# A four-layer diffusion block: two groups of samples per pass of a loop, or four groups in one unrolled wave

## The reference

```python
# L0: ln, modulate, self attention (rope, mask 128x128), gate; ln, cross attention (77 keys, mask), gate; ln, MLP 4x, gate
x = x + g_msa * self_out
x = x + g_x * cross
x = x + g_mlp * (gelu(xm @ W1 + b1) @ W2 + b2)
# L1: ada_ln of x and of the context, cross attention (77 keys)
x = x_q + (out @ Wp + bp)
# L2: self attention gated by gate_msa; cross attention (77 keys); MLP 4x gated by gate_mlp
# L3: nx = ln(x); one-head attention over 77 keys gives evidence
combined = concat(nx, evidence, anchor)
h = silu(combined @ e_w1 + e_b1)              # 3 experts of 256
routed = sum(expert_out * router_probs)
g = sigmoid(silu(combined @ gate_w1 + gate_b1) @ gate_w2 + gate_b2)
x = x + g * (routed @ out_w + out_b)
```

## Time and profile before

| | |
|---|---|
| median of 3 runs | 987.18 us (987.16 to 987.22) |
| the profiled execution | 980.62 us, span 978.7 us |
| mean granted TensorE clock | 0.856 of full |
| PE busy | 780.3 us (80%), 9226 matmuls |
| DVE, ACT, POOL busy | 468.3 us, 325.2 us, 203.1 us |
| instructions | 22436 |

### The profile page before, as it was taken

The page is one execution under the profiler, slowest core; times in us unless marked ns, Lnnn a source line. Parts: engine busy times, 40 slices in busy tenths (PEclk is TensorE's granted clock), DMA queues, the critical chain, the costliest instruction groups (busy, mean ns, idle before and its releaser), DMA issues.

```text
span 978.7 us, 22436 instructions
## 1 busy us (share of the span) xinstructions
PE 780.3 (80%) x9226; PEld 474.7 (49%) x9226; DVE 468.3 (48%) x1111; ACT 325.2 (33%) x544; POOL 203.1 (21%) x239
## 2 busy tenths in 40 slices
PE   5688888787788788868947888878878878887797
PEld 4244444545454455554633445454544445555447
DVE  3557544444455755332146566545344676343403
ACT  0123334233323333325421233352423233224362
POOL 1323221212123322010013233213022223111000
PEclk9799978858778987689979999996777899659899
DMA  8300000000000000000031000000000000000000
GB/s 299 109 1 13 13 1 2 2 1 2 2 2 2 2 2 2 1 0 1 1 109 50 2 3 1 2 1 1 2 1 2 1 2 2 1 2 1 1 0 23
DMA packets 5360, 16.26 MB, mean 17 GB/s; under 512 B 1577, under 2 KB 2612, under 8 KB 4360
## 3 DMA queue, kind: packets, MB, share of 16 engines
q1 hardware_dynamic: 4588, 10.72, 3.3%
q10 hardware_dynamic: 668, 4.05, 1.1%
HBM read 13.66 MB, written 1.09 MB: 15 GB/s over the span
## 4 chain that ended last, share of the span: by engine, by line
PE 65%; ACT 13%; DVE 11%; issue 8%; POOL 1%; DMA 1%; DVEq 0%; SPq 0%; ACTq 0%; POOLq 0%
PE avp L1006 15%; PE lin L889 12%; PE big L981 11%; PE lin L902 10%; ACT P L528 7%; ACT hT L515 4%; PE big L957 3%; DVE mhl L734 2%; PE big L989 2%; PE lin L911 2%; PE big L977 2%; DVE hid L758 2%; PE mtp L963 2%; PE big L974 1%; DVE xn L696 1%
## 5 line engine op out<-in xcount | busy, mean ns | idle before, releaser
L528 ACT ACTIVATE P<-big 77x1024 f32<-77x1024 f32 (+1 forms) x160 | 154.6, 1017 | 406.0 <-PE big L989 406.0
L734 DVE TENSOR_REDUCE mhl<-big 128x8 bf16<-128x616 f32 (+1 forms) x160 | 152.8, 964 | 108.2 <-PE big L957 105.3
L889 PE MATMUL lin<-hT,W 128*128 128x512 f32 x184 | 115.4, 734 | 39.5 <-ACT hT L515 37.0
L469 POOL TENSOR_TENSOR qm<-qT,hm 128x512 f32<-128x512 f32 x80 | 88.6, 1108 | 198.6 <-PE big L989 104.3
L981 PE MATMUL big<-qm,kT 32*77 32x512 f32 (+1 forms) x640 | 111.1, 770 | 0.0
L1006 PE MATMUL avp<-P,Vp 77*32 77x128 f32 (+1 forms) x2560 | 99.7, 304 | 4.0 <-ACT P L528 4.0
L1006 PE MATMUL avp<-P,onesp 77*32 77x128 f32 (+1 forms) x2560 | 101.4, 308 | 0.0
L436 POOL TENSOR_SCALAR rstd<-mv 128x4 f32<-128x4 f32 (+1 forms) x36 | 8.3, 230 | 433.0 <-DVE mv L687 432.8
L957 PE MATMUL big<-kbm,qb 32*128 32x308 bf16 (+1 forms) x320 | 57.4, 359 | 50.4 <-ACT P L528 50.2
L1006 PEld LDWEIGHTS avp<-P,Vp 77*32 77x32 f32 (+1 forms) x2560 | 73.8, 120 | 29.9 <-issue 19.4
L1006 PEld LDWEIGHTS avp<-P,onesp 77*32 77x32 f32 (+1 forms) x2560 | 85.7, 126 | 1.2
(11 more groups left out here) (153 smaller groups left out, 843.2 us busy)
## 6 DMA issues: line engine op xcount, KB each, us to landing
gbc<-gate_rows SPq DMA_DIRECT2D x4, 1280.0 KB, 8.8
W<-in_w ACTq DMA_DIRECT2D x2, 1152.0 KB, 12.3
hid<-in_ws SPq DMA_DIRECT2D x2, 832.0 KB, 5.7
W<-in_w ACTq DMA_DIRECT2D x1, 1088.0 KB, 6.7
xin<-in_x SPq DMA_DIRECT2D x4, 256.0 KB, 4.8
out<-x SPq DMA_DIRECT2D x4, 256.0 KB, 2.2
ctx<-in_ctx SPq DMA_DIRECT2D x4, 154.0 KB
ctxT<-in_ctxT SPq DMA_DIRECT2D x4, 154.0 KB
```

Source lines behind the costliest of these rows:

```text
L469: nc.gpsimd.tensor_tensor(qm[:, j % 2], q.broadcast_to([128, 4, T]), mask.broadcast_to([128, 4, T]), ALU.mult).then_inc(qm_ready, 1)
L528: nc.scalar.activation(P[j % 2][0:kw, 8 * half:8 * half + 8, :], big[0:kw, 2 * half:2 * half + 2, :].rearrange("p g (h q) -> p (g h) q", h=4),
L734: v.tensor_reduce(mhl[:].rearrange("p (g c) -> p g c", c=32)[:, 2 * half:2 * half + 2, 0:4], big[:, 2 * half:2 * half + 2, 0:4 * kw].rearr ...
L889: i = mm(lin_ap(st, s, job, m)[:, 0:n], w, a, start=(c == 0), stop=(c == len(parts) - 1))
```

## The change

The loop is gone: `NS` = 4 groups are in flight, `ITERS` and all turns counted by iteration disappear, and the list `UNITS` is run once. Attention blocks follow each other in `ORDER`, a wave: group 1 begins while group 0 is between its first two blocks, and so on. A chain of side work (`CHAINS`) is laid between two blocks of its group, each unit at a share of the way, over the blocks of the other groups that lie between. `TAILS` lays out the last MLP and the mixture of each group: those of group 0 wholly, of groups 1 and 2 partly, behind attention jobs, the rest behind `END`.

```diff
-NS = 2
-ITERS = B // (GB * NS)
+NS = B // GB
...
+ORDER = [(0, 0), (0, 1), (1, 0), (0, 2), (1, 1), (2, 0), (0, 3), (1, 2), (2, 1), (3, 0),
+         (1, 3), (2, 2), (3, 1), (4, 0), (2, 3), (3, 2), (4, 1), (3, 3), (4, 2), (4, 3)]
+POS = {block: p for p, block in enumerate(ORDER)}
+JOBS = len(ORDER) * GB
+END = 16 * len(ORDER)
...
+CHAINS = [
+    along((0.0, ("l0", "stat")), (0.15, ("l0", "apply")), (0.3, ("l0", "t")), (0.45, ("p0", "k")), (0.7, ("p0", "q")),
+          (1.0, ("p0", "v"))),
+    along((0.0, ("p1", "k"), ("l4", "stat")), (0.1, ("o0", "y")), (0.25, ("l4", "apply")), (0.35, ("l1", "stat"), ("l4", "t")),
+          (0.5, ("p1", "v")), (0.65, ("l1", "apply")), (0.8, ("l1", "t")), (1.0, ("p1", "q"))),
+    along((0.0, ("o1", "y"), ("l2", "stat")), (0.15, ("l2", "apply")), (0.25, ("l2", "t")), (0.35, ("m0", "h0")),
+          (0.38, ("m0", "h1")), (0.42, ("m0", "h2")), (0.46, ("m0", "h3")), (0.56, ("m0", "y"), ("l3", "stat")),
+          (0.6, ("p2", "k")), (0.7, ("p2", "v")), (0.74, ("l3", "apply")), (0.86, ("l3", "t")), (1.0, ("p2", "q"))),
...
+TAILS = [(16 * 14, 16 * 18), (16 * 17, END + 16), (16 * 19, END + 60), (END + 16, END + 76)]
+
+
+def chain_slots(k, s):
+
+    if k == NAT:
+        return TAILS[s]
+    end = 16 * POS[k, s] - 6
+    if k:
+        return 16 * (POS[k - 1, s] + 1), end
+    return max(16 * POS[k, s] - 28, 0), end
...
+def placed():
 
     out = []
+    for s in range(NS):
+        for k, chain in enumerate(CHAINS):
+            if (k, s) == (0, 0):
+                continue
+            first, last = chain_slots(k, s)
+            for share, u in chain:
+                slot = first + round(share * (last - first))
+                if u == (f"p{k}", "v"):
+                    slot = max(slot, values_slot(k, s))
+                    assert slot < 16 * POS[k, s] + 3
+                out.append((slot, u, s))
+    return sorted(out, key=lambda e: e[0])
+
+
+PLACED = placed()
+UNITS = [("B", u, 0) for _, u in CHAINS[0]] + [("START", None, None)]
+for _slot in range(END):
+    UNITS.append(("A", _slot // 4, _slot % 4))
+    UNITS += [("B", u, s) for slot, u, s in PLACED if slot == _slot]
+UNITS += [("END", None, None)] + [("B", u, s) for slot, u, s in PLACED if slot >= END]
```

```diff
+        Vp2 = [sb(f"Vp{i}", [128, GB, H, 32]) for i in range(2)]
+        hid2 = [sb(f"hid{i}", [128, 7, N]) for i in range(2)]
+        Vp, hid = ([pair[s % 2] for s in range(NS)] for pair in (Vp2, hid2))
+        gring = sb("gring", [128, NGB, GB, 128])
...
-        P = [sb(f"P{i}", [128, H, T]) for i in range(2)]
+        P = sb("P", [128, H, T])
...
+            sp.wait_ge(gate_rows_out, 16)
+            for n in range(NGB):
+                gates(n)
+            used = 0
+            for kind, u, s in UNITS:
+                if kind == "B" and u[1] == "y" and u[0] in GATED:
+                    sp.wait_ge(x_ready[s], gated_turn(u[0], s))
+                    if u[0] == "x3":
+                        sp.dma_start(out[:, s * GB:(s + 1) * GB, :], xs[s][:]).then_inc(stored[s], 16)
+                    else:
+                        used += 1
+                        if used + NGB <= len(GATE_USES):
+                            gates(used + NGB - 1)
...
+            def values(a, s):
                 st, kw = f"p{a}", ATT[a]["kw"]
+                earlier = [p for (_, s2), p in POS.items() if s2 % 2 == s % 2 and p < POS[a, s]]
+                if earlier:
+                    dve.wait_ge(av_full, job_turn(max(earlier) * GB + GB - 1))
+                lin_ready(dve, st, s, "v")
...
-                    v.tensor_tensor(t1[s][:, 0, :].rearrange("p (b d) -> p b d", b=GB), y, gate, ALU.mult).then_inc(free, 1)
+                    gy = oT[s][:].rearrange("p (b d) -> p b d", b=GB)
+                    v.tensor_tensor(gy, y, gate, ALU.mult).then_inc(free, 1)
```

More of the change, by code:

```diff
@@ L124 @@
-assert all(a[0] <= b[0] for stages in BETWEEN for a, b in zip(stages, stages[1:]))
-LAST = ([("l7", "t")] + [("m1", f"h{c}") for c in range(4)] + [("m1", "y")] + norm_parts(8)
-        + [("x3", j) for j in X3_PARTS if j not in ("k", "v")])
-JOBS = NAT * NS * GB
-def merge(k, s_att, between, s_bet):
-    out = []
-    for i in range(4 * GB):
-        out.append(("A", (k * NS + s_att) * GB + i // 4, i % 4))
-        out += [("B", u, s_bet) for quarter, u in between if quarter == i]
-    return out
@@ L164 @@
             _n += 1
-LIN_JOBS = _n
-assert LIN_JOBS % 2 == 0
 def lin_bank(st, s, job):
     return LIN_AT[(st, s, job)] % 2
-def lin_turn(it, st, s, job):
-    return it * (LIN_JOBS // 2) + LIN_AT[(st, s, job)] // 2 + 1
-LN_ORDER = [(int(u[0][1:]), s) for kind, u, s in UNITS if kind == "B" and u[1] == "stat"]
-assert all(LN_ORDER == [(int(u[0][1:]), s) for kind, u, s in UNITS if kind == "B" and u[0][0] == "l" and u[1] == part]
-           for part in ("apply", "t")), "a norm's steps are counted in the order of its statistics"
@@ L183, with lin_turn @@
[L183 to L207 removed]
+def lin_turn(st, s, job):
+    return LIN_AT[(st, s, job)] // 2 + 1
@@ new lines, with norm_turn, gated_turn, job_turn @@
+QB_ORDER = [(int(u[0][1:]), s) for kind, u, s in UNITS if kind == "B" and u[0][0] == "p" and u[1] == "q"]
+NGB = 4
+assert all(groups_of(("x3", part)) == groups_of(("x3", "s")) for part in X3_PARTS)
+assert all(groups_of(("p0", part)) == list(range(NS)) for part in "kq")
+def norm_turn(k, s):
+    return LN_ORDER[s].index(k) + 1
+def gated_turn(st, s):
+    return GATED_ORDER[s].index(st) + 1
+def job_turn(j, part=0, per=1):
+    return j * per + part + 1
+def job_of(j):
+    return ORDER[j // GB] + (j % GB,)
@@ new lines, in _ @@
+            for kind, u, s in UNITS:
+                if kind == "START":
+                    act.wait_ge(gate_rows_out, 16)
+                elif kind == "A" and s == 0:
+                    exps(u, 0)
+                    exps(u, 1)
+                elif kind == "B":
+                    st, part = u
+                    k = int(st[1:])
+                    if part == "t":
+                        norm(k, s)
+                    elif st[0] == "p":
+                        project(k, s, part)
+                    elif st[0] == "m" and part != "y":
+                        mlp(k, s, int(part[1:]))
+                    elif st == "x3":
+                        mixture(s, part)
@@ new lines, in mixture @@
+                    lin_taken(dve, st, s, "g")
+                    add_result(st, s, hid[s][:, 5, :].rearrange("p (b d) -> p b d", b=GB))
+            for kind, u, s in UNITS:
+                if kind == "START":
+                    for half in range(2):
+                        maxima(0, half)
+                elif kind == "A":
+                    if s == 0:
+                        turned(u)
+                        if u > 0:
+                            normalise(u - 1)
+                    elif s < 3 and u + 1 < JOBS:
+                        maxima(u + 1, s - 1)
+                elif kind == "END":
+                    normalise(JOBS - 1)
+                elif kind == "B":
+                    st, part = u
+                    k = int(st[1:])
+                    if part == "stat":
+                        statistics(k, s)
+                    elif part == "apply":
+                        apply(k, s)
+                    elif st[0] == "p":
+                        project(k, s, part)
+                    elif st[0] in "om" and part == "y":
+                        if st in gate_of:
+                            n = GATE_USES.index((st, s))
+                            dve.wait_ge(g_in[n % NGB], 16 * (n // NGB + 1))
+                            add_result(st, s, gring[:, n % NGB])
+                        else:
+                            add_result(st, s, None)
+                    elif st == "x3":
+                        mixture(s, part)
@@ L890, in linear, with tokens @@
                 give(st, s, job, i)
[L892 to L894 removed]
+            def tokens(st, s, job, src, wts, bias=None, t=T):
+                take(st, s, job)
                 o = lin_ap(st, s, job, t)
```

614 lines of the change are left out of this document (253 added, 361 removed), and 6 rows, old and new, of the table CHAINS.

## The result

The changed kernel takes 906.1 us (median of 4 runs, 900.8 to 909.9) against 987.2 for the kernel before on the same chip: ratio 0.915, 95% interval 0.908 to 0.923, faster by 81 us. I had said 895, and 845 to 955. The profiled execution has a span of 908.0 us. A median is over all runs of a kernel and a ratio over its fast runs alone, because some executions of any kernel here are a few per cent slower than the rest.

A forecast was written before the change was run, and what follows sets the result against it. TensorE, busiest in every slice with a swinging clock, was taken as the bound: start 42, busy 558.6, idle 86, slow clock 86, finish 115 gave 888 us; with 8.5 outside the span 896, stated as 895, range 845 to 955.

The forecast's parts named there:

- Start: One start instead of two: the 25.5 us restart goes, and the first start falls from 45.4 to about 42 us.
- Busy at full clock: TensorE in the wave of 80 jobs: 374.8 us of attention plus 183.8 of side work, 558.6 us.
- Slow clock: Extra TensorE time in the wave from lowered clock: 15.5% in place of 19.3%, 86 us, bounds 35 and 108.
- rival 3: The clock stays up because the long waits are gone: 822 us, chance 0.12.
- Idle time in the wave: TensorE waits in the wave: 119.6 us bare, 74 hidden by side work, 40 added back, giving 86; bounds 60 and 135.
- (a): TensorE's waits for ACT's `hT` behind norms in the wave, some 28 us over twenty pairs before, now nothing.
- (b): Quarter-3 work, four gated additions and six rotary units, makes DVE late for `turned`: 22 us of idle time in the wave.
- (c): ACT's table loads in the wave cost only at nine places with Gelu or Silu at quarter 3: 7.5 us.
- Finish: One finish instead of two: 87.7 us of side work behind the last attention job, times 1.31, 115 us.
- No cost: ... Unrolling: One `P` buffer, the four-row gate ring, the extra wait in `values` and unrolled loops cost nothing; both passes were fetched already.
- Rival 1: Spreading buys nothing, engines wait as before: idle 135, slow clock 108, finish 119, 971 us; chance 0.13.
- Rival 2: Slower: ACT's queue becomes the wait, exponentials behind Gelu, Silu and reloads, idle 193, 1003 us; chance 0.05.

The follow-up runs named there:

- experiment 12: Kernel of experiment 5 with 8 to 20 more unread matmuls before six late turns and 12 before the mixture's transposes of two groups; 842.1 us, ratio 0.854.
- experiment 5: Changed kernel plus eight unread matmuls before the wait for exponentials in each job without TensorE side work behind quarter 0; 846.3 us, ratio 0.855.
- experiment 3: Changed kernel with 20 norm transposes moved back directly in front of the projections that read them; 967.6 us, ratio 0.981.
- experiment 2: Changed kernel with Gelu, Silu and Sigmoid of the units replaced by Identity, so no table reloads in the list; 889.5 us, ratio 0.896.
- experiment 4: Changed kernel with its groups taken in pairs, one pair after the other, in one list without the stagger; 960.1 us, ratio 0.973.

## Why the prediction was right, and by how much each step

The time came out 11 us from the point and inside the forecast of 860 to 930. The mechanism was the one forecast: norm waits gone, one start and one finish, the clock a little up. The closeness is partly luck: the span was missed by 20 us (888 for 908), and an offset that was 10 too large took half of that back. By its terms, from the profiled run:

**Start.** 43.2 for 42: right.

**Busy at full clock.** 558.6 was worked out from bare jobs and unit prices. Experiment 12 measures it: leave out the records of its fillers, and TensorE was busy 566.1 us in the wave, 10 of them at half clock, so 561 at full; the same working on experiment 5 gives 556. Right to 0.5%, but two errors cancel in it. The rows on `lin` in the wave of experiment 12 take 201.4 us at a clock of 0.99, where I had 183.8 of side work, and the rest 364.7, where I had 374.8 of attention. Rows of both kinds overlap, so a part of this is in how they are counted; how much was not looked at.

**Slow clock.** 641.6 - 561 = 81 us in place of 86 (86 by the 556 of experiment 5). The size was right, and the reason given ("fell behind a norm-to-projection wait ... a bare job then stayed at it") too, but the share was a guess, and I used the mechanism only to trim it. Experiments 3 and 5 show the two sources apart: the norm waits put back add 23 us, and filling the waits for exponentials takes away 68 of the 81. "A bare job has 30% idle time", the reason against rival 3, is what the fillers removed.

**Idle time in the wave.** 98.5 for 86, the step that was most off. Its parts err in both directions. (a) The norm waits: their removal was priced at 28 us, and the two waves before have 29.6 in 20 places: right. (Experiment 3 puts 37.5 back, in longer waits, and 23 of clock with them.) (b) VectorE late was put at 22 beside some 5 left of the maxima's 0.5 us, 27 together; the waits for `mhl` and `mT` are 19 in the wave. I looked for them at quarter 3, and the largest stand behind quarters 0 and 1, where statistics and apply come between two searches for maxima. The exponentials are the other side: of 80 waits of 1.1 us, 88, I let 41 hide behind quarter 0 and 5.6 behind quarter 1, which leaves 41; they took 63.0. Of the 22 us between, 7 are the 0.09 us per job that written-out loops add; the rest I did not divide. (c) Table loads in the wave, 7.5 of idle time: 5.5 by experiment 2, and with the clock 10.2 of time. The forecast had every load for Exp ahead of TensorE's release, and 5 of 13 were not. The loads of the kernel before were miscounted by one: 21 lie behind its start, not 22.

**Finish.** 124.7 for 115, and outside the 108 to 122 that were to show the theory right. The factor 1.31 from the finish before leaves out that three groups there alternate Silu and Gelu: 17 table loads lie in this finish and 6 in each of those before; without any it takes 115.0 (experiment 2, 6.0 of the 9.7 us idle time and the rest work at a clock of 0.97 for 0.94). That this is the very figure forecast is chance, since the factor had 6 loads in it. The count of 48 loads was right; their place in the finish was not looked at.

**"No cost: ... Unrolling".** The reason given, no more fetched, was right: the instruction queue moved 1.21 MB. The conclusion was wrong. It costs some 9 us with the clock held up, and 26 in the old order, where it also lowers the clock. The ring and the single `P` buffer showed no wait among the longest; neither was taken out by a run of its own.

**The rest of the sum.** The terms give 888 and the span is 908: +1 start, -3 busy and clock together, +12 idle, +10 finish. The 8.5 added for what lies outside the profiled span was 10 too much: the median of the runs is 2 below the span here.

**The rivals.** Rival 1 said 971 with idle 135: undo the spreading of the norms alone (experiment 3) and there are 967.6 us with idle 136.0. So the norm waits are what kept it from happening, as argued against it. That both figures meet so closely is chance: experiment 3 has longer norm waits than the kernel before (38.3 us for 29.6). Rival 2 (ACT's queue, 1003) had no sign: loads cost 0.35 to 0.44 us each. Rival 3 (822, clock up) is what fillers nearly reach, 846, while carrying 41 us of them in the wave.

## What to carry to other kernels

Where TensorE's granted clock lies under 1 in a stage, a wait has two prices: its length, and the work behind it at half speed. Here that was 0.6 us for each us of norm wait. So first try matmuls that nobody reads in the waits that can't be removed: 304 of them gave 60 us, three quarters of what a rewrite of the whole order gave, and 464 in the old kernel gave 75 us by themselves. And compare a reordering with such fillers on both sides, since the clock otherwise counts in its favour or against it.

When side work is put under attention, what matters is distance between producer and reader: 20 norms put beside their readers cost 61 us (experiment 3), and one norm whose apply and transposes shared a quarter cost 24 us of idle time in four groups (experiment 4). How much of the 81 us is the stages without attention that went, 27 or more, stays open. Look at each VectorE unit between two of its urgent steps, not only at the last quarter.

## What the runs showed of the hardware

**VectorE's apply beside POOL.** Of the four instructions of 3.24 us above, three ran while POOL worked without a break and took 984, 1077 and 1077 ns; the fourth began as POOL's last instruction ended and took 334. Durations of that instruction in the changed kernel, min/median/max:
```profile
L703 DVE TENSOR_SCALAR xn<-x,mv,rstd x128: 317/340/1077, 26.9 to 847.0; 128x128 f32<-128x128 f32 x128
```
Of the 144 applies (16 are of `ctx`), 21 took over 500 ns, and each of these 21 ended within 0.09 us of the end of an instruction of POOL (the first is at 96.49, 954 ns; the last at 728.79, 736). The 112 that began while POOL was idle took 338 ns on the mean and 346 at most; the 32 that began beside POOL 685. The Trainium skill (GPSIMD Engine Reference, Specifications) has the two engines share their way to SBUF, with contention for some VectorE instructions. The trace agrees in that every slow apply lies beside POOL's work; no run here took that work away to test it.

**Written-out loops.** The wait of scores for exponentials rose from 1.07 to 1.10 us to 1.16 to 1.19 us when the loops were written out, in every bare job looked at. Why a straight program passes this hand-over from ACT to TensorE 0.09 us later than a looped one stays open.

**Half clock lasted where the short waits were bare.** Across waits of 1.15 to 1.2 us TensorE ran at 1.2 GHz for 30.7 us on end (experiment 5). Such waits did not bring the clock down each time: in the changed kernel it stood at full from 54.0 to 159.8 us, across six of them (the window has a clock of 1.00), and fell at 159.8, inside the gap of 3.26 us. What decides between the two is not shown. With fillers in those waits no stretch at 1.2 GHz in the wave was longer than 6.8 us, though the gaps of over 2 us before late maxima stood where they were.
